# Two gated cross-attention and expert layers on one core: an expert stage in four parts, woven into one order of steps

## The reference, cut to what matters

```python
x = x + tanh(g_xattn[0]) * L0_xattn(layernorm(x), ctx)        # 16 heads of 8, rotary q and k
x = x + tanh(g_ffn[0])   * L0_ffn(layernorm(x))               # 8 experts, the best one, relu, gate = its softmax probability
x = x + tanh(g_xattn[1]) * L1_xattn(layernorm(x), ctx, mask)  # 16 heads, biases, key mask
x = x + tanh(g_ffn[1])   * L1_ffn(layernorm(x))               # 8 experts, the best two, silu(x Wg) * (x Wu), softmax over the two
```

## Time and profile before

| what | value |
|---|---|
| runs | 448.67, 449.59, 460.7 us (median 449.59) |
| profiled execution | span 464.2 us, first to last instruction; the page gives no other time for it |
| busy in the span | PE 314.7 us (68%), DVE 264.1 (57%), POOL 152.2 (33%), ACT 136.3 (29%) |
| granted TensorE clock, mean | 0.828 of full speed |
| DMA | 52.93 MB, mean 114 GB/s |

### The profile page before, as it was taken

How to read it: one execution, slowest core, us unless ns; L and a number is a source line. 1 busy time by engine, 2 the same in 40 slices (tenths; PEclk the granted TensorE clock), 3 DMA queues, 4 the chain that set the end, 5 groups by cost and what they waited for, 6 DMA issues and landing times.

```text
span 464.2 us, 7008 instructions
## 1 busy us (share of the span) xinstructions
PE 314.7 (68%) x1932; PEld 228.1 (49%) x1932; DVE 264.1 (57%) x916; ACT 136.3 (29%) x302; POOL 152.2 (33%) x172
## 2 busy tenths in 40 slices
PE   2468999989754095751467999999530298888920
PEld 2236555545353094640256566654320297777820
DVE  2768668773675244353367667765545066665634
ACT  2412354535313033220103454354200033333300
POOL 3211212051423134561102102165766134555550
PEclk9767799999985579795567999999855599999985
DMA  7434032100000867823231313000103677988708
GB/s 268 126 74 118 12 80 52 43 11 19 17 8 29 224 215 215 243 73 90 62 85 36 71 27 85 14 24 23 42 29 100 213 244 236 299 249 289 235 12 269
DMA packets 39997, 52.93 MB, mean 114 GB/s; under 512 B 7177, under 2 KB 24334, under 8 KB 39968
## 3 DMA queue, kind: packets, MB, share of 16 engines
q1 hardware_dynamic: 33648, 45.03, 33.7%
q0 software_dynamic: 3584, 6.36, 3.9%
q10 hardware_dynamic: 2736, 1.20, 0.9%
HBM read 35.58 MB, written 9.64 MB: 97 GB/s over the span
## 4 chain that ended last, share of the span: by engine, by line
PE 21%; DVE 8%; issue 7%; DMA 6%; SPq 4%; POOL 4%; ACT 1%; POOLq 0%; DVEq 0%; ACTq 0%
POOL routed L445 3%; PE ps_s L750 2%; PE ps_a L730 2%; DMA xt<-routed 2%; PE ps_a L731 2%; PE ps_s L821 2%; SPq L342 2%; PE ps_s L751 2%; PE ps_t L705 2%; PE ps_n L765 2%; PE ps_a L838 1%; PE ps_d L765 1%; PE ps_t L821 1%; DMA probs<-expert_out 1%; DMA routed<-pay,slot 1%
## 5 line engine op out<-in xcount | busy, mean ns | idle before, releaser
L463 POOL DMA_INDIRECT expert_out<-yo,rows_at x64 | 63.0, 984 | 81.5 <-DVE yo L1179 63.6
L529 ACT ACTIVATE probs<-ps_s 103x512 f32<-103x512 f32 (+1 forms) x96 | 56.3, 597 | 56.8 <-PE ps_s L751 53.3
L445 POOL DMA_INDIRECT routed<-pay,slot x48 | 48.4, 1009 | 58.3 <-DVE slot L1132 47.8
L1025 DVE TENSOR_REDUCE negm<-ps_a 128x4 f32<-128x308 f32 x128 | 55.1, 470 | 19.5 <-PE ps_a L731 18.0
L750 PE MATMUL ps_s<-qs,ks 128*103 128x512 f32 (+1 forms) x96 | 46.2, 481 | 2.0 <-ACT augT L522 1.2
L731 PE MATMUL ps_a<-ks,qs 128*128 128x308 f32 x128 | 43.1, 374 | 5.9 <-DVE negm L1025 5.6
L421 POOL TENSOR_SCALAR ve<-mv 128x4 f32<-128x4 f32 x16 | 4.0, 251 | 116.0 <-DVE mv L975 116.0
L751 PE MATMUL ps_s<-augT,aug 128*103 128x512 f32 (+1 forms) x96 | 39.6, 412 | 0.0
L838 PE MATMUL ps_a<-cst,xt 128*128 128x128 f32 x32 | 11.1, 355 | 39.8 <-DMA xt<-routed 38.2
L731 PEld LDWEIGHTS ps_a<-ks,qs 128*128 128x128 f32 x128 | 28.9, 227 | 15.4 <-DVE negm L1025 6.6
L821 PE MATMUL ps_s<-xT,probs 128*128 128x128 f32 x208 | 32.5, 299 | 2.9 <-DVE xT L1190 1.7
(11 more groups left out here) (168 smaller groups left out, 659.3 us busy)
## 6 DMA issues: line engine op xcount, KB each, us to landing
probs<-f_in SPq DMA_DIRECT2D x40, 384.0 KB
qs<-qhl SPq DMA_DIRECT2D x128, 64.0 KB, 2.0
probs<-f_in SPq DMA_DIRECT2D x24, 321.0 KB
xt<-routed SPq DMA_DIRECT2D x32, 65.0 KB
probs<-routed SPq DMA_DIRECT2D x32, 65.0 KB
...
```

Of the source, the lines that this page charges most:

```text
L445: pool.indirect_dma_start(out=routed[l], out_offset=bass.IndirectOffsetOnAxis(ap=slot[c][:, t:t + 1], axis=0), in_=pay[c][:, t, :], in_off ...
L463: pool.indirect_dma_start(out=expert_out[l], out_offset=bass.IndirectOffsetOnAxis(ap=rows_at[i % SHORT][:, :], axis=0), in_=yo[i % SHORT][ ...
L529: nc.scalar.activation(probs[n % 2][0:KSIZE[j], s, :], ps_s[(NS * n + s) % SCORE_BANKS][0:KSIZE[j], :], ACT.Exp, scale=SCALE).then_inc(exp ...
L1025: nc.vector.tensor_reduce(negm[:, i, g * HPG:(g + 1) * HPG], a[:, 0:GK].rearrange("p (h k) -> p h k", h=HPG), AX.X, ALU.max, negate=True). ...
```

## The change

**Parts.** The expert stage of each layer is cut in two parts of two batches, four streams in all: 15, 15, 23 and 23 tiles (76 instead of 64), with a plan, row region and run of counts for each.

**One order.** There is one list of steps for both layers, from -28 to 220; `START` gives each batch's first score step. Tables say at which step a stream's plan, weights, rows, tiles and results stand. The tiles of part 0 of layer 0 (steps 53 to 67, `up` and `down` up to 70) stand between the stages of batches 2 and 3's tails; part 1 (73 to 87) between the front stages of batches 4 and 5, which are batches 0 and 1 of layer 1; the second layer's first scores are step 105; its two parts stand at 163 to 185 and 186 to 208. Nothing is a loop any more. A stretch is `calm` when no scores are near; all tile steps are, and `up` then uses the two score banks, `down` the two banks `ps_n` and `ps_d`. `claim` makes PE wait until the last user of a bank has read it.

**Pad rows.** `pad_rows` and its transfers are gone. Two regions of 8192 rows are filled once from the cosine table by 16 POOL transfers of 532 KB (`fill`), a half in steps 4 to 11 and a half in 20 to 27. `limit` computes per tile which rows are past the count, and `finish` gives these an out-of-range row number.

**Memory and others.** `probs` has one copy; weights have 7 slots of their own, rows 8. Layer 1's keys are made at step 16 and spread at step 62; `take_keys` masks straight from PSUM (4 operations per group) and `mask_keys` is gone. `SET_UP_AT` is -18 (before -14), `normalise2` 21 steps after the start (before 23).

The diff, cut to its core:

```diff
+PARTS = [[(0, 1), (2, 3)], [(0, 1), (2, 3)]]
+STREAMS = [(l, p) for l in range(LAYERS) for p in range(len(PARTS[l]))]
+CAP = [len(PARTS[l][p]) * SEQ for l, p in STREAMS]
+BLOCKS = [cap // P for cap in CAP]
+T = [(cap * CHOICES[l] + E * (P - 1)) // P for (l, p), cap in zip(STREAMS, CAP)]
+FIRST_TILE = [sum(T[:g]) for g in range(len(T))]
...
+W_SLOTS, X_SLOTS, SHORT = 7, 8, 4
+FILL, FILLS = 4 * PAY, 8
...
-    "results": -30, "stats": -26, "normalise": -25, "bias": 9, "turn": -22, "project": -20, "high": -19, "low": -19,
-    "split": -3, "augment": -2, "weigh0": 5, "weigh1": 9, "weigh2": 13, "sums": 13, "den": 15, "widen": 15, "rden": 17,
-    "output": 18, "stats2": 19, "normalise2": 23, "turn2": 23, "router": 25, "route_exp": 26, "ranks": 28,
-    "scatter0": 29, "scatter1": 31, "scatter2": 34, "scatter3": 35,
+    "results": -28, "stats": -28, "normalise": -25, "bias": 12, "turn": -22, "project": -20, "high": -19, "low": -19,
+    "split": -3, "augment": -2, "weigh0": 5, "weigh1": 9, "weigh2": 13, "sums": 13, "den": 14, "widen": 16,
+    "rden": 18, "output": 19, "stats2": 20, "normalise2": 21, "turn2": 23, "router": 25, "route_exp": 26, "ranks": 28,
+    "scatter0": 30, "scatter1": 30, "scatter2": 36, "scatter3": 34,
...
-MAX_UNITS = [1, 2, 2, 2, 1, 2, 2, 2, 1, 1]
+MAX_UNITS = [2, 1, 3, 0, 2, 2, 2, 2, 1, 1]
...
+START = [0, 12, 24, 36, 105, 117, 131, 144]
+FRONT_SHIFT = [0, -6, 0, 0, 0, -6, 0, -2]
...
+KEYS_AT = [-21, 16]
+KEYS_SPREAD_AT = [-18, 62]
+VALUES_AT = [[-2, -1, 0], [54, 57, 58]]
+SET_UP_AT = -18
+FILL_AT = [4, 20]
+PLAN_AT = [41, 66, 152, 176]
+TILES_AT = [53, 73, 163, 186]
+WEIGHTS_AT = [42, 67, 156, 177]
+ROWS_AT = [48, 72, 159, 182]
+BACK_AT = [76, 101, 195, 218]
+FINAL_AT = [196, 197, 219, 220]
+PUT_LAG = 6
...
+def turned(t, lag, count=1):
+
+    return [FIRST_TILE[g] + j for g in range(len(STREAMS)) for j in range(T[g]) if TILES_AT[g] + j + lag == t]
+
...
+def calm(t):
+
+    return all(not -2 <= t - START[n] <= NS for n in range(BATCHES))
+
...
-        probs = [sb(f"probs{i}", [P, NS, SEQ]) for i in range(2)]
+        probs = sb("probs", [P, NS, SEQ])
+        fws = sb("fws", [P, W_SLOTS * max(FW)])
...
-        up_bank = [*ps_s, *ps_a[2:], ps_t]
...
+            def load_weights(m):
+
+                g = stream(m)
+                l = STREAMS[g][0]
+                if m == FIRST_TILE[g]:
+                    sp.wait_ge(meta_ok, g + 1)
+                at = offsets(m, 0, (E - 1) * P * FW[l])
+                if m >= W_SLOTS:
+                    sp.wait_ge(f_y, m - W_SLOTS + 1)
+                sp.dma_start(fw[m % W_SLOTS][:, 0:FW[l]], f_in[l].rearrange("e p f -> (e p f)")[bass.ds(at, P * FW[l])].rearrange("(p f) -> p f", p=P)).then_inc(f_w[m % W_SLOTS], 16)
+            def load_rows(m):
+
+                g = stream(m)
+                l, p = STREAMS[g]
+                at = offsets(m, 1, (E * BLOCKS[g] - 1) * P * PAY)
+                if m == FIRST_TILE[g]:
+                    for n in PARTS[l][p]:
+                        sp.wait_ge(scattered[n % 2], scattered_by(NB * l + n))
+                if m >= X_SLOTS:
+                    sp.wait_ge(f_y, m - X_SLOTS + 1)
+                sp.dma_start(xt[m % X_SLOTS][:, :], routed[p].rearrange("k c -> (k c)")[bass.ds(at, P * PAY)].rearrange("(p c) -> p c", p=P)).then_inc(f_r[m % X_SLOTS], 16)
...
+            def fill(p, q):
+
+                pool.wait_ge(ld_c, 16)
+                rows = routed[p].rearrange("k c -> (k c)").rearrange("(q p k c) -> q p k c", q=FILLS, p=P, c=FILL)
+                pool.dma_start(rows[q], bcast(cst[:, C_COS:C_COS + FILL], 1, rows.shape[2])).then_inc(filled, 16)
...
+            def put(m):
+
+                l = STREAMS[stream(m)][0]
+                pool.wait_ge(f_y, m + 1)
+                pool.indirect_dma_start(
+                    out=expert_out[l], out_offset=bass.IndirectOffsetOnAxis(ap=rows_at[m % SHORT][:, :], axis=0),
+                    in_=yo[m % SHORT][:, :], in_offset=None, bounds_check=last_row[l], oob_is_err=False).then_inc(f_put[m % SHORT], 16)
...
-                if n >= 2 and s == 0:
-                    act.wait_ge(pv_ok, KT * (n - 1))
-                nc.scalar.activation(probs[n % 2][0:KSIZE[j], s, :], ps_s[(NS * n + s) % SCORE_BANKS][0:KSIZE[j], :], ACT.Exp, scale=SCALE).then_inc(exp_ok, 1)
+                if n and g == 0:
+                    act.wait_ge(pv_ok, KT * (n - 1) + j + 1)
+                nc.scalar.activation(probs[0:KSIZE[j], s, :], ps_s[(NS * n + s) % SCORE_BANKS][0:KSIZE[j], :], ACT.Exp, scale=SCALE).then_inc(exp_ok, 1)
...
+                    for h in range(HPG):
+                        last = nc.scalar.activation(ks[:, g, :, h * KEYS:(h + 1) * KEYS], ps_s[0][:, 0:NB * KEYS].rearrange("p (b k) -> p b k", b=NB),
+                                                    ACT.Copy, scale=hm[:, h:h + 1])
+                    last.then_inc(k_even, 1)
...
+            def claim(bank, user, value):
+
+                if bank in held:
+                    pe.wait_ge(*held[bank])
+                held[bank] = (user, value)
...
+                if calm(t):
+                    claim(("s", m % 2), f_hid, m + 1)
+                    bank = ps_s[m % 2]
+                else:
+                    bank = ring("up", m)
...
+            def limit(g):
+
+                nt = T[g]
+                dve.wait_ge(meta_ok, g + 1)
+                link(nc.vector.tensor_tensor(le[:, 0:nt, :], bcast(ej[:, 0:nt], 2, E), bcast(cst[:, C_IOTA:C_IOTA + E], 1, nt), ALU.is_equal))
+                link(nc.vector.tensor_tensor(let[:, 0:nt, :], le[:, 0:nt, :], bcast(counts[:, :], 1, nt), ALU.mult))
+                link(nc.vector.tensor_reduce(bj[:, 0:nt], let[:, 0:nt, :], AX.X, ALU.add))
+                link(nc.vector.scalar_tensor_tensor(kj[:, 0:nt], kj[:, 0:nt], -float(P), bj[:, 0:nt], ALU.mult, ALU.add))
+                link(nc.vector.tensor_scalar(past[g][:, :], kj[:, 0:nt], cst[:, C_ROW:C_ROW + 1], float(NOROW), ALU.is_le, ALU.mult))
...
+                row = xt[m % X_SLOTS]
+                nc.vector.scalar_tensor_tensor(rows_at[m % SHORT][:, :], row[:, D:D + 1].bitcast(I32), float(NOROW), past[g][:, j:j + 1], ALU.min, ALU.max)
...
+                for m in turned(t, PUT_LAG):
+                    put(m)
```

More of the change, by code:

```diff
@@ L117, in bcast, with settled, by_act @@
+def calm(t):
+    return all(not -2 <= t - START[n] <= NS for n in range(BATCHES))
+def settled(t):
+    return all(not AT["weigh0"] - 1 <= t - START[n] <= AT["sums"] for n in range(BATCHES))
+def by_act(key):
+    l = STREAMS[stream(key[1])][0] if key[0] in ("xT", "up") else None
+    return key[0] == "xT" and l == 1 or key[0] == "up" and l == 0
+RING_KEYS = ring_keys()
+RING_AT = {key: u for u, key in enumerate(RING_KEYS)}
 def bcast(ap, axis, n):
@@ L306, in next, with results, scattered_by @@
                 return self.n - 1
-        def rounds(eng, l, body):
-            body(0, True)
-            with eng.Fori(1, FT[l] // SLOTS) as r:
-                body(r, False)
+        def results(n):
+            return [n] if n < NB else [NB + 2 * (n - NB) + c for c in range(2)]
+        def scattered_by(n):
+            return 16 * TPB * sum(CHOICES[k // NB] for k in range(n % 2, n + 1, 2))
         @block.sync
@@ L389, in _ @@
[L389 to L398 removed]
+            values = {}
```

997 lines of the change are left out of this document (509 added, 488 removed).

## The result

The changed kernel takes 458.5 us (median of 6) against 449.85 (6 runs): a ratio of 1.013, 95% interval 1.008 to 1.018. A second set beside other runs of the kernel before gave 1.017 (1.010 to 1.024). The forecast was 405, with a range of 384 to 430. The change makes the kernel 1 to 2% slower, which is clear of the noise though under 2%, and the forecast missed by 53 us.

A forecast was written before the change was run, and what follows sets the result against it. It took TensorE to bound the score stretches, tile stretches as mixed and the rest as dependent chains the change fills. Stage terms summed to 418.1 against 464.2 us; the factor 0.901 on the 449.59 median gave 405, range 384 to 430.

The forecast's parts named there:

- Start, -2.0: Before the first score: masking keys straight from PSUM and an earlier cast save 2.0 us, ends 0 and -3.9; score at 38.2.
- Layer 0 scores, 80.8: Layer 0's score stretch keeps its 80.8 us: -2 for the earlier second normalisation, +2 for fills making q spreads late.
- rival 3: Layer 0 scores: the fills hold back the q spreads, up to 15.6 us; chance 0.10.
- Tail, 36: Layer 0's last score to last slots, 11 tile steps woven in: 36 us, ends 27.3 and 49.7.
- rival 2: Both layers' tails add fully to the tiles, since engines wait in order: 448.3 us, which is 434; chance 0.15.
- POOL's ten issues, 18.4: Last slots to part 1's first tile: 4 scatters and 6 tile puts take 12.8 us, then rows; tile at 173.4.
- Layer 1 scores, 79.3: Layer 1's score stretch: 78.3 us, -2 for the normalisation, +3 for results standing behind a q spread on SyncE.
- First tile 9.7 us behind the scores: Layer 1's tiles begin beside the last output product, 9.7 us after the scores, at 310.0.
- rival 4: Up-projection with two PSUM banks instead of four waits for DVE: 2.8 us per step, 486, which is 471; chance 0.05.
- To the last result, 44.6: Layer 1's part 1: 23 tiles at 1.85 us without a loop, +2 for the first half's results; ends at 402.9.
- rival 1: The tails disappear in the tiles: slots after 27.3 us, tiles at PE's 1.68, free fills; 391.8, which is 379; chance 0.17.
- rival 5: Overlap not had: part 1's rows come so late only start and end gains remain; about 455, which is 441; chance 0.03.

The follow-up runs named there:

- second profile: Another profiled execution of the changed kernel, nothing altered, at a higher granted clock than the first; span 455.8 us against 465.6.
- small_fill: Changed kernel with two blocks per expert filled, not eight, a quarter of the fill bytes; ratio 1.001 to the kernel before.
- late_tiles: mend with layer 0's part 0 tiles behind that layer's tail, part 1's directly behind them, layer 1 12 steps later; 454.39 us, ratio 1.011.
- mend: Changed kernel with full fills moved, batches 2 and 3's results earlier, batch 3's scatters together, layer 1's first plan and loads earlier; 442.07 us, ratio 0.974.
- mend_dense: mend with layer 1's batches 12 steps apart as in the kernel before, what follows three steps earlier; 438.76 us, ratio 0.969.
- plan_early: Changed kernel with layer 1's first plan at step 148 instead of 152, its first weight loads and rows earlier too; ratio 1.005.
- mend_xslots: mend with twelve row buffers instead of eight, so a tile's rows are asked for seven steps ahead instead of three; ratio 0.967.

## Why the prediction was wrong

Of the 53 us, 37.7 are the stages of the sum (455.8 in the second profile against 418.1). Another 13 come from its last step, which carried the factor 0.901 from a profile of 464.2 us to a median of 449.59, as if every stage of that long execution were too long in the same proportion; no run shows this. The rest, 2.7, is the time against the span. By the steps of the prediction:

- **Start, -2.0: not had** (+2.4). The first score is at 40.6, and was at 40.2. Its zero end was the right one.
- **Layer 0 scores, 80.8: 90.7** (+9.9). The step "I take +2" for the fills failed. They cost 8 (small_fill), within the 15.6 of rival 3 (the fills hold back the q spreads, to which I gave 0.10) and near the 8.2 that I had as the end for two late halves; only the first half was late for PE. I treated them as bandwidth with slack behind them; the rows show the pieces of one spread issued and landed late beside fill bytes, a wait of 3.4 to 3.6 us, and the lower clock behind it (0.50 from 66 to 70 us in the second profile). The landing is late by the bytes in flight, at most 8.3 us against 3.7 with a quarter of them; by what mechanism the fills hold back the pieces, no run shows. The "-2" for the normalisation was 0 in layer 0.
- **Tail, 36: 42.2** (+6.2). Without tiles it is 29.5 (late_tiles) against 41.1 in `mend`, which has the same tail with the tiles in it, so the 11 tile steps cost 11.6 us, 1.05 each, where I took 0.79 (8.7). Mechanism right, size between forecast and rival 2's 49.7. Part of it is the clock, which the sum had nowhere: 37.2 us at 0.91 in `mend_dense`, 41.4 at 0.79 in `mend`, with the same steps.
- **POOL's ten issues, 18.4: 19.8.** Right in cause and size. What I didn't see is that it could be undone.
- **Front of layer 1, 24.3 and 23.3: 25.1 and 23.4.** Right.
- **Layer 1 scores, 79.3: 86.9** (+7.6). The step failed at its first word: "78.3" is the length of 48 steps with scores, but the new starts leave 51 steps, three of them without. They cost 5.7 to 8.4 (mend_dense). It stood in the order, and I didn't count it. The results' wait, priced at +3, was 3 against the second profile. The normalisation's -2 was -2.7.
- **First tile 9.7 us behind the scores: 16.9** (+7.2). I took PE's last output product as the release and left out the loads: rows behind 2.7 MB of weights. plan_early gives 5.0 of it back.
- **First 23 tiles, 48.3: 46.7.** Right; rival 4, the two up-projection banks, is refuted: a tile takes 2.03 us here (46.7 / 23), not 2.8, and PE's longest kind of wait in the last tiles is for rows, not for `hid`.
- **To the last result, 44.6: 50.5** (+5.9). The step "1.85" failed: it assumed that only PE and a loop turn set the pace, and the tiles run at 2.05 with PE waiting for transfers. 242 GB/s stood in the earlier trace rows and I used it for the fills alone; at 514 KB per tile it gives an estimate of 2.1 us. Whether the transfers or the weight buffers set the 2.05 stays open (mend_xslots).
- **End, 15.2: 13.0.** 2.2 better.

So the idle chains were filled, but gave less than planned. From layer 0's last score to layer 1's first it is 110.5 us against 126.4 before, 15.9 of the 24.4 forecast, just past the 15 below which the prediction called itself wrong; from layer 1's last score to the last tile result 114.1 against 120.3, 6.2 of 17.7. The terms that failed are the fills (8), the three empty steps (6 to 8), the loads behind weights (5), the denser tail (6) and the tiles' pace (6). No rival held all of it: rival 3, the fills, named the largest single one, and rival 2 part of one; rival 1 is out with a tail of 42 us, rival 5 with part 1's first tile only 20 us behind the slots. 458.5 us lies at the upper edge of what I called within 2%, to which I gave 0.06, with 0.06 more for slower: too little for a sum of ten terms, most of which assumed that a moved thing stays hidden. The curing kernels move the ratio from 1.017 to 0.969, about two fifths of the promised way to 0.901.
